# Two attention stages and the join between them: query chunks outermost, three of four chunks joined inside the first attention, units issued ahead of weighted sums in the second

## The chip, the core and the metric

The kernel runs on one core of a Trainium2 chip. The core has TensorE (matmuls into eight PSUM banks), VectorE, ScalarE, GpSimd and SyncE, each with its own instruction stream; semaphores order them. The metric is the device time of one execution in microseconds, the median of three.

## The reference, cut to what matters

```python
# x: (1, 2048, 128) f32; everything f32
xn = layernorm(x)
# s: first attention, 16 heads of 8, relu instead of softmax, no mask
qkv = xn @ w_qkv                       # per head: q, k, v of 8 columns each
w = relu(q @ k.T / sqrt(8));  w = w / (sum(w) + 1e-6)
y = xn + (w @ v, heads joined) @ w_out + b_out
s = (y - mean(y)) * rsqrt(var(y) + 1e-5) * gamma + beta
# g: a routed transformer block over 255 selected tokens
g = silu(routed_block(xn))
x = x + s * g
xn = layernorm(x)
# s: second attention, 16 heads of 64, causal softmax
q, k, v = xn @ W_Q + b_Q, xn @ W_K + b_K, xn @ W_V + b_V
s = sum over heads of softmax(causal(q @ k.T / 8)) @ v @ W_O, + b_O
# FFN with int32 weights, HIDDEN = 384
g = silu((silu(xn @ w_gate.T) * (xn @ w_up.T)) @ w_down.T)      # weights scaled by 1/127
return x + s * g
```

## The kernel before

Five functions run one after the other, each a block in which every engine has its own program: `prepare`, `routed0`, `attention0`, `between`, `attention1`. The 2048 tokens are 16 tiles (T) of 128, or 4 chunks (NC) of 512 (C = 512 columns, one PSUM bank). Activations stay in SBUF throughout: `sh.x` the residual, `sh.xa` the normalized input, `sh.g` the gate.

**First attention (`attention0`).** Heads are in four groups of four (G = GH = 4). q and k of a group sit in `q_rows` and `k_rows`, copied from DRAM in 16 loads of 128 KB a group by `load_rows` (a load is one `dma_start` at L246 or L249). Group 0 was loaded in `routed0`; groups 1 to 3 are loaded by SyncE at the start of this block, ahead of the weights for the join. A turn is one group and one chunk of queries, 16 turns, group outermost; a step is one tile of 128 keys, 16 steps a turn. In a step TensorE fills two pairs of banks with scores (`scores(s, 0)` and `(s, 1)`, L346), pairs taken from a ring of three, and then adds the weighted sums of the step two earlier (`weigh(s - LAG)`, L363). Of each pair ScalarE makes one relu tile (L406), VectorE the other (L434):

```python
if n >= RING:
    pe.wait_ge(act_relu, n - RING + 1)
    pe.wait_ge(dve_relu, n - RING + 1)
```

Once a turn ScalarE copies the summed output of the turn before (`copy_out`, L397), TensorE turns it by four transposes (L372), and VectorE divides by the sums in three small instructions (`divide`, L418 to L423). GpSimd copies the v columns of each group (two buffers) and folds `beta`, `gamma` and `b_out` into `sh.x`, `sh.g` and `sh.xa`.

**Join and FFN (`between`).** Everything waits for the last turn. TensorE turns the attention's output back (16 matmuls against the identity), ScalarE copies it, TensorE multiplies by `w_out`; VectorE adds `sh.xa` and takes the moments of all 16 tiles, ScalarE takes one square root (L1101), VectorE refines it by a Newton step (`rsqrt_refine`, L65), ScalarE scales 16 tiles (L1124), GpSimd multiplies by `sh.g` and adds to `sh.x` (L1144). Then the second layernorm in two halves, in the same manner, and per chunk four transposes, a split of the turned input in a high and a low part (`x_high`, `x_low`), three gate units (L1082), the multiply into `inner` (L1197), the down projection (L1062) and the last silu (L1118).

**Second attention (`attention1`).** Eight laps, one pair of heads each. A lap has 40 steps (query chunk and tile of 128 keys, causal), in ten groups of four (PER = 4). Units are what fills a pair of banks from a ring of three: `scores` (L1525, L1528), `maximum` (scores once more for the row maxima, L1477, L1482, taken by VectorE at L1687), `turn` and `project`, `value`, `mix`, the "whole" units of the next chunk or lap. `MAXIMA` says how many maxima a group holds, `WHOLE` which whole units. TensorE, ScalarE and VectorE all walk this list; TensorE's loop is

```python
for k in range(GROUPS):
    for unit in rows_phase(k):       # scores and maxima
        fill(unit)
    if k - 1 in ENDS:
        total(ENDS.index(k - 1))
    for s in range(k * PER, (k + 1) * PER):
        weigh(s)                     # weighted sums of the four steps
    for unit in whole_phase(k):
        fill(unit)
```

ScalarE does the exponentials (L1630) and the high parts of projections (`k_hi`, L1609), VectorE the low parts (`k_lo` L1676, `q_lo` L1679) and, after each of a lap's four query chunks, the reciprocal of the row sums and the product with it (`scale`, L1708 and L1711). GpSimd adds up the exponentials (L1444) and sets masks and constants at the start of the block (from L1391 on), which TensorE waits for before its first unit.

Of the kernel before, what the change touches and what calls it, by code (L numbers as in the profile page):

```python
# [15 lines left out]
P = 128  # L16
# [223 lines left out]
def load_rows(sp, sh, group, q_rows, k_rows, loaded):  # L240

    for h in range(GH):
        head = slice((group * GH + h) * HD0, (group * GH + h + 1) * HD0)
        for n in range(PARTS):
            rows = slice(h * ROWS0 + n * PARTS * HD0, h * ROWS0 + (n + 1) * PARTS * HD0)
            sp.dma_start(q_rows[rows, :].bitcast(F32),  # L246
                         sh.parts_dram[0, n, head, :].unsqueeze(0).to_broadcast([PARTS, HD0, S]))\
                .then_inc(loaded, 16)
            sp.dma_start(k_rows[rows, :].bitcast(F32), sh.parts_dram[1, :, head, :]).then_inc(loaded, 16)  # L249


def attention0(nc, a, sh):

    with ExitStack() as ctx:
# [7 lines left out]
        NB = 2  # L262
# [4 lines left out]
        q_rows = [sh.q_rows] + [sb(f"q_rows{n}", [P, S], F32R) for n in range(1, G)]  # L267
        k_rows = [sh.k_rows] + [sb(f"k_rows{n}", [P, S], F32R) for n in range(1, G)]
        v_cols = [sh.v_cols] + [sb(f"v_cols{n}", [P, T, GH, VW]) for n in range(1, NB)]
        w = sb("w0", [P, WR, GH, C])  # L270
        o_sb = sb("o_sb", [P, C])
        den = sb("den", [P, TC, GH])
        beta_g = sb("beta_g", [P, T, D])

        rows_loaded = [sh.rows_loaded] + [sem(f"rows_loaded{n}") for n in range(1, G)]
        fold_step = sem("fold_step")
        v_copied = sem("v_copied")
# [7 lines left out]
        out_done = sem("out_done")  # L285

        bank = sh.bank
        pair_bank = [bank[2 * n:2 * n + 2] for n in range(RING)]
        out_bank = bank[2 * RING:2 * RING + 2]

# [3 lines left out]
        def _(sp):  # L294

            for group in range(1, G):
                load_rows(sp, sh, group, q_rows[group], k_rows[group], rows_loaded[group])
# [6 lines left out]
            sp.dma_start(sh.w_int[:, 2, :], a["L1_ffn_w_down"]).then_inc(sh.join_loaded, 16)  # L304

        @block.gpsimd
        def _(pool):
# [5 lines left out]
            def fold():  # L313

                pool.wait_ge(sh.join_loaded, 16 * 7)
                link(nc.gpsimd.tensor_tensor(beta_g[:, :, :], sh.g[:, :, :], row(2), ALU.mult))
                link(nc.gpsimd.tensor_tensor(sh.x[:, :, :], sh.x[:, :, :], beta_g[:, :, :], ALU.add))
                link(nc.gpsimd.tensor_tensor(sh.g[:, :, :], sh.g[:, :, :], row(1), ALU.mult))
                link(nc.gpsimd.tensor_tensor(sh.xa[:, :, 0:D], sh.xa[:, :, 0:D], row(0), ALU.add))

            for n in range(1, NB):
                nc.gpsimd.memset(v_cols[n][:, :, :, HD0 + 1:VW], 0.0)
                nc.gpsimd.memset(v_cols[n][:, :, :, HD0:HD0 + 1], 1.0)
            for group in range(1, G):
                if group == NB:
                    fold()
                if group >= NB:

                    pool.wait_ge(weighted, (group - NB + 1) * NC * T)
                heads = sh.v0[:, :, group * GH * HD0:(group + 1) * GH * HD0]  # L330
                nc.gpsimd.tensor_copy(v_cols[group % NB][:, :, :, 0:HD0],
                                      heads.rearrange("p t (h j) -> p t h j", j=HD0)).then_inc(v_copied, 1)

        @block.tensor
        def _(pe):
            def scores(s, m):

                turn, kt = divmod(s, T)
                group, qc = divmod(turn, NC)
                n = 2 * s + m  # L340
                if n >= RING:
                    pe.wait_ge(act_relu, n - RING + 1)
                    pe.wait_ge(dve_relu, n - RING + 1)
# [6 lines left out]
            def weigh(s):  # L350
                turn, kt = divmod(s, T)
                group = turn // NC

                pe.wait_ge(act_relu, 2 * s + 2)
                pe.wait_ge(dve_relu, 2 * s + 2)
                if kt == 0:
                    if turn % NC == 0 and group:
# [1464 lines left out]
```

## Time and profile before

| | us |
|---|---|
| median of three runs | 1516.79 |
| the three runs | 1518.03, 1516.79, 1513.65 |
| the profiled execution | 1512.94 |
| its span | 1511.10 |
| TensorE busy | 1343.0 (89%) |
| VectorE busy | 1066.3 (71%) |
| ScalarE busy | 713.9 (47%) |
| GpSimd busy | 690.5 (46%) |

The span is the time from the first to the last instruction of the profiled execution; the 1.84 us between it and that execution's own time lie around the program. The busy times are averages over stages with different limits: the first attention runs from 158.3 to 545.9 us, the join and FFN to 618.3, the second attention to the end, and each is read by itself. The granted TensorE clock is a share of full speed. The chain of work that ended last runs over TensorE for 41% of the span, VectorE 10%, GpSimd and ScalarE 3% each.

### The profile page before, as it was taken

To read this page: it belongs to the slowest core of one execution; us is meant where nothing else is said; L and a number is where in the kernel's file an instruction comes from. 1 tells how busy PE (TensorE), PEld (TensorE's weight loads), DVE (VectorE), ACT (ScalarE), POOL (GpSimd) and SP (SyncE) were. 2 spreads that over 40 slices of the span, in tenths; PEclk is the share of its full clock that TensorE was granted. 3 is DMA by queue.
4 is the path that set the end of the run, shared out by engine and by line. 5 is a ranking of instruction groups with operands and counts; after the bars stand their busy time and mean duration, and the time that the engine had idled before them with its cause. 6 is when DMAs were issued, how large, how long until landed. Compare 5 with 4: busy or idle time off the path is not lost.

```text
span 1511.1 us, 25889 instructions
## 1 busy us (share of the span) xinstructions
PE 1343.0 (89%) x10066; PEld 700.4 (46%) x10066; DVE 1066.3 (71%) x1631; ACT 713.9 (47%) x1134; POOL 690.5 (46%) x485
## 2 busy tenths in 40 slices
PE   5398999999999964598999999999999999999894
PEld 3377322222222233455555555555555555555552
DVE  6774788888888866377676586586676765765853
ACT  2043677777777753333434434444434344344431
POOL 1100000400000002155777777877777777777785
PEclk9598999999999997999999999999999999999997
DMA  5100111100000010000000000000000000000000
GB/s 183 65 8 0 41 54 59 40 1 2 2 1 2 2 43 1 16 1 1 1 2 1 1 1 1 1 1 1 1 1 1 1 1 1 2 1 1 8 8 14
DMA packets 18183, 21.59 MB, mean 14 GB/s; under 512 B 7672, under 2 KB 15888, under 8 KB 16528
## 3 DMA queue, kind: packets, MB, share of 16 engines
q1 hardware_dynamic: 18064, 19.94, 3.8%
q8 instruction: 82, 1.34, 0.4%
q14 instruction: 37, 0.30, 0.1%
HBM read 14.70 MB, written 5.24 MB: 13 GB/s over the span
## 4 chain that ended last, share of the span: by engine, by line
PE 41%; DVE 10%; POOL 3%; ACT 3%; issue 1%; POOLq 0%; DVEq 0%; ACTq 0%
PE psum L1547 14%; PE psum L1525 11%; PE psum L1477 4%; DVE part_max L1687 4%; PE psum L1528 3%; POOL acc L1444 3%; PE psum L1509 2%; DVE inv L1708 2%; ACT prob L1630 2%; PE psum L1500 2%; DVE k_lo L1676 2%; ACT k_hi L1609 1%; DVE q_lo L1679 1%; PE psum L1464 1%; PE psum L1455 1%; PE psum L1457 1%
## 5 line engine op out<-in xcount | busy, mean ns | idle before, releaser
L1444 POOL TENSOR_TENSOR acc<-acc,prob 128x1024 f32<-128x1024 f32 (+3 forms) x264 | 525.3, 1990 | 91.3 <-ACT prob L1630 59.9
L1687 DVE TENSOR_REDUCE part_max<-psum 128x2 f32<-128x1024 f32 (+2 forms) x320 | 334.9, 1064 | 105.5 <-PE psum L1477 81.1
L1630 ACT ACTIVATE prob<-psum 128x1024 f32<-128x1024 f32 (+1 forms) x320 | 283.0, 897 | 210.7 <-PE psum L1528 205.5
L434 DVE TENSOR_SCALAR w<-psum 128x512 f32<-128x512 f32 x512 | 328.1, 686 | 49.8 <-PE psum L346 33.6
L406 ACT ACTIVATE w<-psum 128x512 f32<-128x512 f32 x512 | 278.0, 596 | 102.7 <-PE psum L346 102.5
L363 PE MATMUL psum<-w,v_cols 128*32 128x512 f32 x2048 | 273.6, 607 | 0.0
L1547 PE MATMUL psum<-prob,v_pair 128*64 128x512 f32 (+3 forms) x1280 | 251.3, 535 | 5.7 <-POOL prob L1414 5.7
L1525 PE MATMUL psum<-q_hi,k_hi 64*128 64x512 f32 (+3 forms) x640 | 138.8, 429 | 34.0 <-DVE q_lo L1679 23.0
L1547 PEld LDWEIGHTS psum<-prob,v_pair 128*64 128x64 f32 x1280 | 87.8, 137 | 148.8 <-issue 130.2
L1477 PE MATMUL psum<-k_hi,q_hi 64*128 64x512 f32 (+3 forms) x640 | 129.3, 402 | 16.2 <-DVE max_rows L1702 5.5
L1708 DVE RECIPROCAL inv<-psum 128x512 f32<-128x512 f32 x32 | 107.4, 3355 | 28.2 <-PE psum L1500 27.9
L1525 PE MATMUL psum<-q_hi,k_lo 64*128 64x512 f32 (+3 forms) x640 | 117.9, 363 | 0.0
L1525 PE MATMUL psum<-q_lo,k_hi 64*128 64x512 f32 (+3 forms) x640 | 117.8, 362 | 0.0
L1528 PE MATMUL psum<-max_rows,ones_r 64*128 64x512 f32 (+3 forms) x640 | 117.6, 362 | 0.0
L346 PEld LDWEIGHTS psum<-q_rows,k_rows 32*128 32x128 f32 x768 | 41.0, 181 | 156.3 <-ACT w L406 148.7
L346 PE MATMUL psum<-q_rows,k_rows 32*128 32x512 f32 x768 | 104.6, 493 | 0.0
L1525 PEld LDWEIGHTS psum<-q_hi,k_hi 64*128 64x128 f32 x640 | 60.2, 184 | 89.8 <-DVE q_lo L1679 31.1
L1144 POOL TENSOR_TENSOR y<-y,g 128x512 f32<-128x512 f32 x4 | 5.1, 1265 | 210.5 <-ACT y L1124 210.5
L1414 POOL TENSOR_SCALAR_AFFINE_SELECT prob<-prob 128x256 f32<-128x256 f32 x128 | 51.8, 406 | 107.1 <-ACT prob L1630 106.0
L1477 PEld LDWEIGHTS psum<-k_hi,q_hi 64*128 64x128 f32 x640 | 60.6, 185 | 63.1 <-ACT prob L1630 36.3
L1609 ACT ACTIVATE k_hi<-psum,bias 128x512 fp32r<-128x512 f32 x32 | 22.0, 689 | 122.5 <-PE psum L1457 122.5
L1440 POOL TENSOR_TENSOR acc<-prob 128x1024 f32<-128x1024 f32 x24 | 57.3, 2386 | 32.0 <-ACT prob L1630 30.4
(268 smaller groups left out, 1460.5 us busy)
## 6 DMA issues: line engine op xcount, KB each, us to landing
parts_dram<-parts SPq DMA_DIRECT2D x4, 1024.0 KB, 4.7
q_rows<-parts_dram SPq DMA_DIRECT2D x24, 128.0 KB
k_rows<-parts_dram SPq DMA_DIRECT2D x24, 128.0 KB
x<-in_L_attn_x SPq DMA_DIRECT2D x4, 256.0 KB, 3.9
mask<-in_L_ffn_attention_mask SPq DMA_DIRECT2D x1, 1024.0 KB, 5.4
x_high<-parts_dram SPq DMA_DIRECT2D x8, 128.0 KB
x_low<-parts_dram SPq DMA_DIRECT2D x8, 128.0 KB
out<-xa SPq DMA_DIRECT2D x4, 256.0 KB, 2.3
```

The lines of the kernel that those rows point to most:

```text
L346: last = nc.tensor.matmul(pair_bank[n % RING][i], k_rows[group][rows, kt * P:(kt + 1) * P], q_rows[group][rows, qc * C:(qc + 1) * C], star ...
L363: last = nc.tensor.matmul(out_bank[turn % 2][h * VW:(h + 1) * VW, :], v_cols[group % NB][:, kt, h, :], w[:, s % WR, h, :], start=(kt == 0) ...
L406: nc.scalar.activation(w[:, s % WR, 2 * m, :], pair_bank[n % RING][0], ACT.Relu)\
L434: nc.vector.tensor_scalar(w[:, s % WR, 2 * m + 1, :], pair_bank[n % RING][1], 0.0, None, ALU.max)\
L1444: nc.gpsimd.tensor_tensor(sums, sums, prob[:, s % PR, :, q0:C], ALU.add).then_inc(summed, 1)
L1477: last = nc.tensor.matmul(to[:, m, 0:n], q_hi[HALF[m], i * P:(i + 1) * P], k_hi[hp % 2][HALF[m], c * C:c * C + n], start=True, stop=not di ...
L1525: nc.tensor.matmul(to[:, m, q0:C], left[HALF[m], keys], right[HALF[m], at], start=n == 0, stop=False)
L1528: last = nc.tensor.matmul(to[:, m, q0:C], ones_r[HALF[m], :], max_rows[HALF[m], at], start=False, stop=True)
L1547: last = nc.tensor.matmul(out_bank[HALF[m], q0:C], v_pair[hp % 2][:, kt, HALF[m]], prob[:, s % PR, m, q0:C], start=kt == 0, stop=kt == (qc ...
L1630: nc.scalar.activation(prob[:, s % PR, :, q0:C], unit_both[n % RING][:, :, q0:C], ACT.Exp, scale=SCALE)\
L1687: nc.vector.tensor_reduce(part_max[:, :, i, c], unit_both[n % RING][:, :, 0:cols], AX_X, ALU.max)\
L1708: nc.vector.reciprocal(inv[:, :], side_bank).then_inc(inv_done, 1)
```

## The change

**Row loads.** Group 1 is loaded in `routed0` by SyncE, behind the other loads of that block. In `attention0` SyncE loads group 3 alone, and ScalarE's program begins with the 16 loads of group 2. The loads of the second attention's head weights, of `row_o` and of `wo` move from later blocks to the end of SyncE's list in `attention0`.

```diff
         @block.sync
         def _(sp):
-            for group in range(1, G):
-                load_rows(sp, sh, group, q_rows[group], k_rows[group], rows_loaded[group])
+            load_rows(sp, sh, 3, q_rows[3], k_rows[3], rows_loaded[3])
...
+            load_heads_start(sp, a, sh)
...
         @block.scalar
         def _(act):
+            load_rows(act, sh, 2, q_rows[2], k_rows[2], rows_loaded[2])
```

ScalarE's instructions at the start of the first attention, before (the two branches open the block, `w` are relu tiles):

```order
L444 UNCONDITIONAL_BRANCH
L390 UNCONDITIONAL_BRANCH
L406 ACTIVATE w<-psum 128x512 x36
L397 COPY o_sb<-psum 128x512
L406 ACTIVATE w<-psum 128x512 x32
```

and after (the two DMA rows stand there eight times in turn):

```order
L593 UNCONDITIONAL_BRANCH
L499 UNCONDITIONAL_BRANCH
L246 DMA q_rows<-parts_dram 16x1x2048
L249 DMA k_rows<-parts_dram 16x1x2048
...
L529 ACTIVATE w<-psum 128x512 x37
L508 COPY o_sb<-psum 128x512
L529 ACTIVATE w<-psum 128x512 x34
```

Sixteen DMAs stand ahead of the first relu, and the rows of 32 relu tiles a turn have become 34.

**Turns.** The query chunk is outermost, the group innermost, so that a chunk has all its heads after four turns. v columns have a buffer for each group. In listed steps (`SPARE`) ScalarE makes both relu tiles of the step's second pair and VectorE none: the divide step, step 12 of each turn, and the steps in which VectorE works for the join. The waits count accordingly.

```diff
-                group, qc = divmod(turn, NC)
+                qc, group = divmod(turn, G)
                 n = 2 * s + m
                 if n >= RING:
-                    pe.wait_ge(act_relu, n - RING + 1)
-                    pe.wait_ge(dve_relu, n - RING + 1)
+                    pe.wait_ge(act_relu, ACTS[n - RING])
+                    pe.wait_ge(dve_relu, DVES[n - RING])
...
+        DIVIDE = LAG + 2
+        TURN_O, COPY_O, MIX_O = 7, 8, 10
+        SUM, STATS, VARIANCE, REFINE = 11, (15, 19), 22, 26
+        STATS_X, VARIANCE_X, REFINE_X = (38, 42), 46, 50
+        JOIN = {turn * T: turn // G - 1 for turn in range(G, TURNS, G)}
+        AFTER = {s: (c, s - first) for first, c in JOIN.items() for s in range(first, first + G * T)}
+        DVE_FULL = (SUM,) + STATS + (REFINE,) + STATS_X + (REFINE_X,)
+        SPARE = [s for s in range(STEPS)
+                 if s % T == DIVIDE and s >= T or s in AFTER and AFTER[s][1] in DVE_FULL or s % T == 12]
+        ON_ACT = [2 * s + 1 for s in SPARE]
```

**Joins inside.** For the chunks 0, 1 and 2 the join runs within the next chunk's turns, at the offsets of the list above in steps from the turn's start: transposes (TensorE), a copy (ScalarE), the product with `w_out` (TensorE), sum and moments, a square root (ScalarE), the Newton step (VectorE), the scaling, the product with `sh.g` and the sum (GpSimd, `join_result`), then the second layernorm in the same way.

```diff
+            def turn_rows(c):
+                pe.wait_ge(out_done, (c + 1) * G)
+                for j in range(TC):
+                    last = nc.tensor.transpose(out_bank[1][:, j * P:(j + 1) * P], sh.o0[:, c % 2, j, :], sh.ident[:, :])
...
+            def mix(c):
+                pe.wait_ge(oT_done, c + 1)
+                pe.wait_ge(folded, 1)
+                for j in range(TC):
+                    last = nc.tensor.matmul(out_bank[1][:, j * P:(j + 1) * P], oT[:, j * P:(j + 1) * P], sh.w_out[:, :],
...
+def join_refine(nc, link, sh, n, at, scaled):
+    rsqrt_refine(link, nc, sh.rstd[:, n, at], sh.root[:, n, at], sh.var_eps[:, n, at], sh.newton[:, at])
+    return nc.vector.scalar_tensor_tensor(out=sh.shift[:, n, at], in0=sh.moments[:, n, at, 0], scalar=-1.0,
...
+def join_result(nc, link, sh, c, x_done):
+    for t in range(c * TC, (c + 1) * TC):
+        last = nc.gpsimd.tensor_scalar(sh.xa[:, t, 0:D], sh.xa[:, t, 0:D], sh.rstd[:, 0, t:t + 1],
+                                       sh.shift[:, 0, t:t + 1], ALU.mult, ALU.add)
+    link(last)
+    link(nc.gpsimd.tensor_tensor(sh.xa[:, at, 0:D], sh.xa[:, at, 0:D], sh.g[:, at, :], ALU.mult))
+    nc.gpsimd.tensor_tensor(sh.x[:, at, :], sh.x[:, at, :], sh.xa[:, at, 0:D], ALU.add).then_inc(x_done, 1)
```

GpSimd also runs `second_constants` there, the masks, `ident_b`, `ones_r` and `own_tile` of the second attention.

**`between`.** Only the last chunk is joined here. Its chain (copy, transposes, divide, transposes, copy, product, sum, square root, scaling on GpSimd, second layernorm) is interleaved with the FFN of chunks 0 to 2; chunk 3's FFN ends the block. TensorE's order, in the names of the new code:

```diff
+            turn_xn(0)
...
+            turn_xn(1)
...
+            gate(0, 0)
...
+            gate(0, 1)
+            gate(0, 2)
+            turn_xn(2)
+            for f in range(F1T):
+                gate(1, f)
+            down(0)
+            for f in range(F1T):
+                gate(2, f)
+            down(1)
+            turn_xn(3)
+            down(2)
+            for f in range(F1T):
+                gate(3, f)
+            down(3)
```

ScalarE from the weights' copies in this block on, before:

```order
L1095 COPY wT<-psum 128x384
L1101 ACT_TABLE_LOAD
L1101 ACTIVATE root_j<-var_eps_j 128x16
L1124 ACTIVATE y<-y,shift_j,rstd_j 128x128 x16
L1101 ACTIVATE root_j<-var_eps_j 128x8 x2
L1131 CAST w_high<-w_heads 128x2048
L1105 CAST x_high<-psum 128x512
L1106 COPY xnT<-psum 128x512
L1111 ACT_TABLE_LOAD
L1111 ACTIVATE act_gate<-psum 128x512 x3
```

and after:

```order
L1277 COPY wT<-psum 128x384
L1279 COPY o0T_last<-psum 128x512
L1262 ACT_TABLE_LOAD
L1262 ACTIVATE act_gate<-psum 128x512
L1254 CAST x_high<-psum 128x512
L1255 COPY xnT<-psum 128x512
L1262 ACTIVATE act_gate<-psum 128x512 x2
L1250 ACT_TABLE_LOAD
L1250 ACTIVATE root_j<-var_eps_j 128x4
...
L1262 ACT_TABLE_LOAD
```

The sixteen scalings (`y`) are gone from ScalarE, and square roots alternate with silu, each change of function behind a table load.

**Second attention.** The constants' wait on TensorE is gone. Whole units come ahead of the weighted sums, and of everything that follows a chunk's end:

```diff
             for k in range(GROUPS):
                 for unit in rows_phase(k):
                     fill(unit)
+                for unit in whole_phase(k):
+                    fill(unit)
                 if k - 1 in ENDS:
                     total(ENDS.index(k - 1))
                 for s in range(k * PER, (k + 1) * PER):
                     weigh(s)
-                for unit in whole_phase(k):
-                    fill(unit)
```

The same exchange is made on ScalarE (ahead of `copy_out`) and VectorE (ahead of `scale`). `MAXIMA` becomes 3, 5, 2, 5, 5, 2, 5, 5, 5, 3 instead of four a group; `PLACES` says where in a group they stand (mostly one ahead of each score unit), and `WHOLE` is dealt anew. `neg_max` gets two buffers.

VectorE around one scaling in the first full lap, before:

```order
L1687 TENSOR_REDUCE part_max<-psum 128x2 x4
L1708 RECIPROCAL inv<-psum 128x512
L1711 TENSOR_TENSOR z<-z,inv 128x512
L1676 SCALAR_TENSOR_TENSOR k_lo<-psum,bias,k_hi 128x512
L1679 SCALAR_TENSOR_TENSOR q_lo<-psum,bias,q_hi 128x512
L1687 TENSOR_REDUCE part_max<-psum 128x2 x4
L1695 TENSOR_REDUCE neg_max<-part_max 128x2x4
```

and after:

```order
L1829 TENSOR_REDUCE part_max<-psum 128x2 x5
L1818 SCALAR_TENSOR_TENSOR k_lo<-psum,bias,k_hi 128x512
L1821 SCALAR_TENSOR_TENSOR q_lo<-psum,bias,q_hi 128x512
L1850 RECIPROCAL inv<-psum 128x512
L1853 TENSOR_TENSOR z<-z,inv 128x512
L1829 TENSOR_REDUCE part_max<-psum 128x2 x5
L1837 TENSOR_REDUCE neg_max<-part_max 128x2x4
```

The reciprocal and its product stood ahead of the low parts and now stand behind them, right in front of the next maxima.

## Rows read from the trace of the kernel before

**Rows 1.** Windows: stretch, length, busy (instructions) by engine, clock, DMA share, GB/s.

```profile
158.30:254.70 96.40, 95.51 (x766) 24.83 (x767) 83.14 (x137) 70.28 (x131) 1.97 (x3) 0.98 0.13 53
...
544.70:618.30 73.60, 38.28 (x345) 31.19 (x341) 37.25 (x126) 28.43 (x54) 9.99 (x8) 0.81 0.10 23
...
858.60:964.80 106.20, 100.56 (x734) 59.02 (x732) 72.26 (x68) 44.85 (x56) 80.03 (x54) 1.00 0.00 1
```

**Rows 2.** Timeline, first attention: start, us, engine, line, operation, out<-in, [idle before <-releaser].

```profile
188.32 0.66 PE L372 MATMUL psum<-ident,o_sb 128*128 128x128 f32 x4
...
190.73 0.16 DVE L418 TENSOR_SCALAR den<-psum 128x16 f32<-128x16 f32 x1
...
191.42 2.47 DVE L434 TENSOR_SCALAR w<-psum 128x512 f32<-128x512 f32 x4
...
191.79 0.95 PE L346 MATMUL psum<-x_high,x_low 32*128 32x512 f32 x4
...
193.67 0.51 PE L346 MATMUL psum<-x_high,x_low 32*128 32x512 f32 x4
...
195.10 0.52 PE L346 MATMUL psum<-x_high,x_low 32*128 32x512 f32 x4
...
195.71 1.08 ACT L406 ACTIVATE w<-psum 128x512 f32<-128x512 f32 x2 [0.35 <-PE psum L346]
```

**Rows 3.** Timeline of SyncE's queue, first attention.

```profile
158.30 0.62 SPq L246 DMA_DIRECT2D q_rows<-parts_dram  x1
...
165.36 2.12 SPq L249 DMA_DIRECT2D k_rows<-parts_dram  x1
...
173.96 2.11 SPq L249 DMA_DIRECT2D k_rows<-parts_dram  x1
...
253.05 2.11 SPq L249 DMA_DIRECT2D k_rows<-parts_dram  x1
```

**Rows 4.** Timeline of the join and FFN, all engines.

```profile
545.94 0.58 ACT L397 COPY o_sb<-psum 128x512 f32<-128x512 f32 x1 [1.60 <-PE psum L363]
...
553.89 1.28 ACT L1101 ACT_TABLE_LOAD   x1
...
562.33 0.25 DVE L65 RECIPROCAL rstd_j<-root_j 128x16 f32<-128x16 f32 x1 [0.28 <-ACT root_j L1101]
...
563.66 6.26 ACT L1124 ACTIVATE y<-y,shift_j,rstd_j 128x128 f32<-128x128 f32 x16 [1.37 <-DVE shift_j L1176]
...
565.39 1.26 POOL L1144 TENSOR_TENSOR y<-y,g 128x512 f32<-128x512 f32 x1 [210.53 <-ACT y L1124]
...
590.87 2.94 PE L1062 MATMUL psum<-wT,inner 128*128 128x128 f32 x24 [0.97 <-DVE inner L1197]
...
594.58 0.40 PE L1082 MATMUL psum<-x_high,wT_int 128*128 128x512 f32 x1
...
594.81 0.40 PE L1082 MATMUL psum<-x_low,wT_int 128*128 128x512 f32 x1
```

**Rows 5.** Timeline, start of the second attention, TensorE.

```profile
625.94 0.77 PE L1455 MATMUL psum<-x_high,w_high 128*128 128x512 f32 x1 [7.18 <-POOLq L1407]
```

**Rows 6.** Who waited for whom, one lap, 858.6 to 964.8: total us, times, longest.

```profile
PEld psum L1477 <- ACT prob L1630: 5.0, 14, 0.5
...
PEld psum L1525 <- DVE q_lo L1679: 4.6, 4, 1.3
PEld psum L1525 <- DVE part_max L1687: 3.9, 12, 0.7
...
PEld psum L1477 <- DVE max_rows L1702: 1.2, 1, 1.2
```

**Rows 7.** Timeline of VectorE in the same lap.

```profile
903.19 3.36 DVE L1708 RECIPROCAL inv<-psum 128x512 f32<-128x512 f32 x1
906.58 1.97 DVE L1711 TENSOR_TENSOR z<-z,inv 128x512 f32<-128x512 f32 x1
...
913.26 1.23 DVE L1687 TENSOR_REDUCE part_max<-psum 128x2 f32<-128x1024 f32 x1 [0.17 <-PE psum L1477]
```

More of the change, by code:

```diff
@@ new lines, in turn_xn, with gate @@
+                    last = nc.tensor.transpose(bank[c][:, j * P:(j + 1) * P], sh.xa[:, c * TC + j, 0:D], sh.ident[:, :])
+                last.then_inc(xn_turned, 1)
+            def gate(c, f):
+                n = c * F1T + f
+                if f == 0:
+                    pe.wait_ge(x_low_done, c + 1)
+                if n == 0:
+                    pe.wait_ge(wT_done, 3)
+                if n == 1:
+                    pe.wait_ge(out_done, 1)
+                if n >= 2:
+                    pe.wait_ge(inner_done, n - 1)
+                for m in range(2):
+                    for part in (sh.x_high, sh.x_low):
+                        last = nc.tensor.matmul(gate_bank[n % 2][m], wT_int[:, m, f * P:(f + 1) * P],
+                                                part[:, c * C:(c + 1) * C], start=part is sh.x_high,
+                                                stop=part is sh.x_low)
+                last.then_inc(gate_done, 1)
@@ new lines, in _ @@
+            turn_xn(1)
+            pe.wait_ge(out_done, 1)
+            for j in range(TC):
+                last = nc.tensor.transpose(bank[LAST][:, j * P:(j + 1) * P], sh.o0[:, LAST % 2, j, :], sh.ident[:, :])
+            last.then_inc(o_turned, 1)
+            gate(0, 0)
+            pe.wait_ge(oT_done, 1)
+            for j in range(TC):
+                last = nc.tensor.matmul(bank[LAST][:, j * P:(j + 1) * P], oT[:, j * P:(j + 1) * P], sh.w_out[:, :],
+                                        start=True, stop=True)
@@ L1088, in _, with deviation @@
+            last.then_inc(projected, 1)
+            gate(0, 1)
[12 more added lines that the diff above has]
+            down(3)
         @block.scalar
         def _(act):
-            for c in range(NC):
-                act.wait_ge(turned, c + 1)
-                nc.scalar.copy(oT[:, c * C:(c + 1) * C], bank[c]).then_inc(oT_done, 1)
+            def deviation(n):
+                at = slice(LAST * TC, T)
+                act.wait_ge(var_done, n + 1)
+                nc.scalar.activation(sh.root[:, n, at], sh.var_eps[:, n, at], ACT.Sqrt).then_inc(root_done, 1)
@@ L1128, in _ @@
-            for m in range(PARTS_X):
-                deviation(1, m)
+            act.wait_ge(o_turned, 1)
+            nc.scalar.copy(oT[:, :], bank[LAST]).then_inc(oT_done, 1)
+            gate(0, 0)
+            take_xn(1)
+            gate(0, 1)
+            gate(0, 2)
+            deviation(0)
+            take_xn(2)
+            for f in range(F1T):
+                gate(1, f)
+            gate(2, 0)
+            finish(0)
+            deviation(1)
+            gate(2, 1)
+            gate(2, 2)
@@ L1194, in multiply @@
[L1194 to L1204 removed]
+            at_last = slice(LAST * TC, T)
@@ L1653, in _ @@
                     take(unit)
+                for unit in whole_phase(k):
+                    take(unit)
                 if k in ENDS:
                     copy_out(ENDS.index(k))
-                for unit in whole_phase(k):
-                    take(unit)
         @block.vector
```

584 lines of the change are left out of this document (315 added, 269 removed).

## The prediction, made before the changed kernel had run

> **What bounds the kernel now.** I read the windows by stage first, then the timeline inside each stage, then who waited for whom. The program is four stages in a row: preparation and the routed block to 158.3 us, the first attention from 158.3 to 545.9, the join with its FFN to 618.3, the second attention to the end. In the two attention stages TensorE is busy nearly all the time; in the join its busy share is 38.28 of 73.60 us and its granted clock 0.81 [rows 1]. That stage is a chain through all engines, not a load.
>
> In the first attention a step is two pairs of score tiles, four relu tiles and one set of weighted sums. TensorE sets the pace: steps start 1.43 us apart (193.67 to 195.10). Once a turn of 16 steps there are two longer ones: the output transposes at 188.32 add some 0.6 us, and the step from 191.79 to 193.67 takes 1.88, 0.45 too much, because VectorE has just done the three divide instructions that begin at 190.73 beside its two relu tiles, at 0.62 to 0.69 us each [rows 2]. VectorE is busy 83 of 96 us there and ScalarE 70 [rows 1].
>
> The row loads from DRAM are cheap only because SyncE has nothing else to do. SyncE issues 48 of them: the first eleven take 0.6 us each, from the twelfth on each issue is held 2.1 us or longer, and the 16th is through at 176.07, 17.8 us after the start. From 165.36 to 253.05 are 36 loads, 2.43 us each [rows 3]. The DMA share of that window is 0.13 of 16 engines, so about two engines carry all of it [rows 1].
>
> In the second attention a lap of one head pair takes 106.2 us, with GpSimd busy 80 [rows 1]. TensorE's queue stood 14.7 us of it: 5.0 for ScalarE's exponentials, 4.6 for the low part of a projection, 3.9 for VectorE's maxima, 1.2 for spread maxima [rows 6].
>
> **The change part by part.** The sum is made against the profiled execution, 1512.94 us (span 1511.10 and 1.84 around it). The median of the three runs shown is 3.85 higher; I carry the difference over to it.
>
> (a) Sixteen row loads, of group 2, now stand on ScalarE's own queue ahead of its first relu, while SyncE issues the 16 of group 3. No row shows a DMA issued by ScalarE, so this is bounded. By SyncE's rows, a 16th issue completes when seven loads have drained: 7 x 2.43 = 17.0, and 17.8 was seen [rows 3]. If ScalarE's loads drain through the same two engines as SyncE's, taking turns, seven of its own are 14 in all: 14 x 2.43 = 34 us. I take this, because two engines carried all loads though they go to different partitions and some nine of them were queued; that speaks for the shape of the transfer choosing the engines. Less the 0.6 us after which ScalarE's first relu started before, it is **+33**. Nothing covers it: TensorE can fill three pairs of banks, then it waits for ScalarE. The other ends are 16 x 0.62 = 9.9 us if no queue fills, and 23 x 2.43 = 56 if both queues share one stock of nine loads. A short hold would not be all gain: all 32 loads need 78 us on two engines, and turn 2, which reads group 2, would come 50 us after the first relu.
>
> The Trainium skill, "DMA: Bandwidth & Descriptors", section "Why a DMA increments its semaphore by 16 and not by 1", says that a transfer from SyncE or ScalarE runs on the lowest-numbered k engines, k following from the slowest dimensions, and both engines' DMAs run on the same 16 ("Issuing engines are not separate DMA queues"). By that rule sharing is sure. The trace agrees so far, with its two busy engines. That last section also says that a second issuer saves "the time on the sequencer it takes to initiate the DMA, which is usually small relative to the DMA itself"; by that the hold would be small and the time rival B's. SyncE's 2.11 us speaks against it.
>
> (b) The rest of the first attention. ScalarE takes both tiles of a pair in the divide step, so VectorE does one relu less where it divides (2.47/4 = 0.62 us against the 0.69 from 190.73 to 191.42, [rows 2]): 15 stalls of 0.45 go, -6.8. ScalarE has that time (0.35 us idle in a 1.43 us step, [rows 2]), and its late tile is wanted only two steps later. Three of four chunks are now joined inside: on TensorE four transposes (0.6) and four fp32 matmuls, eight passes at 2.94/24 = 0.12 [rows 4], about 1.0: 3 x 1.6 = +4.7. On VectorE the sum and the statistics are covered by the relu tiles given away; the two refinements a chunk take 1.33 us each (562.33 to 563.66, [rows 4]) against one tile of 0.62, the two variances about 0.6 against none. Where a divide of 0.69 cost 0.45, I take 0.3 for each of these 12: +3.5, between 0 and 7. One activation table load (1.28, [rows 4]) before the first square root: +1. Together **+2**. GpSimd's part and the SyncE loads behind it lie beside relu work.
>
> (c) The join and FFN take 618.3 - 545.9 = 72.4 us now: 545.94 is ScalarE's copy after the last weighted sums [rows 4], 618.3 the next block. The first down projection starts only at 590.87, 45 us in. After the change three chunks are normalized already and only the last goes through the chain, beside the FFN of the others. I follow it from the last weighted sum: copy, transposes and divide 3 us; its transposes behind nine weight transposes, one gate unit (four matmuls 0.23 apart, [rows 4]) and the mixing: 6; sum and statistics 9; square root behind a table load 10.7; refinement 13; four scalings and two products of 1.26 on GpSimd [rows 4] 17; second statistics 18.6; second root, behind two table switches and the first down projection, 22.2; 23.5; GpSimd 25; transposes 25.5; ScalarE's w_high and copies 28.4; three gate units and their multiplies 34.6; down 2.94; last activation and block end: 38.4. I add 2.5 for VectorE instructions beside GpSimd and for a TensorE clock that may sink again. 41 against 72.4: **-31**, from -36 to -27. ScalarE loads five tables here instead of two; two of the three extra ones are in this chain.
>
> (d) Constants of the second attention are set during the first. TensorE's first projection waited 7.18 us for them and then ran at the lower clock (0.77 us instead of 0.40 for a matmul) [rows 5]. The wait goes, and about 1 us of slow matmuls: **-8**.
>
> (e) Units in front of weighted sums. A projection now has 3.5 us of weighted sums behind it while ScalarE and VectorE split it, so the 4.6 and the 1.2 of [rows 6] go. But VectorE now meets the reciprocal last: 3.36 us, then a product of up to 1.97 [rows 7], start only after the whole units, and the next group's maxima stand behind them. In the group after a scaling, with q_lo done 2.3 us after the projection (k_hi, k_lo and q_lo in a row), the scaling ends 7.0 to 7.6 after it and the weighted sums 4.6: 2.4 to 3 us late. With 1.23 us a maximum and a ring of three bank pairs, the second score unit waits for the first maximum, so this lateness becomes TensorE's. I get 2.4, 1.2, 2.4 to 3 and 1.3 us for the four scalings of a lap, but the usual 0.8 of such a group is in them: about +5 net. Five maxima in full groups and two or three in diagonal ones about even out. 5.8 against 5: per lap nothing within 1.5, over eight laps **0, from -12 to +14**.
>
> Sum: 33 + 2 - 31 - 8 + 0 = -4 us: 1508.9 for the profiled run, **1513** by the median.
>
> **The rivals.** A, ScalarE's loads drain beside SyncE's on other engines: held 17.8 us, 16 less, 1497. Against it is the 0.13 share [rows 1]. A2, the second attention gains 2 us a lap: GpSimd is busy 80 of 106, so there is room [rows 1], and a late maximum may fall into a place where TensorE waited for ScalarE anyway (5.0, [rows 6]): 1497. B, no queue fills: 9.9 us of issue, on other engines, 1489; SyncE's twelfth load [rows 3] speaks against it. C, slower: the reciprocal behind the whole units costs more than the projections give back. Place: the group after each scaling; price 2 us a lap, 1529; it decides once the first maximum after a scaling starts over 3 us after its matmuls. D, slower: the two queues share one stock of queued loads, the hold is 56 us, 1535; it decides when ScalarE's issues are held before its tenth. That the change doesn't do what it says would be the divide stalls and the 7.18 wait still standing; the order of instructions leaves no room for it.
>
> **How the numbers follow.** A measurement here tells about 0.3%, 4.6 us, from no change. Forecast 0.40, with its own range 1505 to 1521; A 0.17; A2 0.13; B 0.04; C 0.16; D 0.07; 0.03 elsewhere. The forecast lies on the border: of its 0.40, 0.18 are faster by over 4.6 us, 0.16 within, 0.06 slower. Faster 0.18 + 0.16 + 0.12 + 0.04 + 0.01 = 0.51; within 0.19; slower 0.30. The range 1488 to 1534 leaves out D and the tails.
>
> **What would show it.** Right: ScalarE's first relu 30 to 37 us after the first attention's start, two DMA engines busy till then; no 1.88 us steps in a turn; 38 to 44 us from the last weighted sums of the first attention to the second attention's block, its first projection within 1 us of it; laps of 105 to 108 us, with no wait for q_lo and longer ones for maxima after each reciprocal. Wrong: a first relu before 20 us or after 50, laps under 104 or over 108, or waits of TensorE for the square roots' chain.

## The result and the profile after

| | before | after |
|---|---|---|
| median, us | 1515.22 | 1497.99 |
| ratio, with its 95% interval | | 0.9892, 0.9862 to 0.9922 |
| profiled execution, us | 1512.94 | 1502.96 |
| its span | 1511.10 | 1501.2 |

The change makes the kernel 1.1% faster, 17 us by the medians. The profiled execution of after is its slowest: the other three took 1496.8 to 1498.5. By stage of the two profiled executions (from the last weighted sums of the first attention, and from the first projection of the second):

| stage | before | after | difference |
|---|---|---|---|
| preparation and routed block | 158.3 | 164.6 | +6.3 |
| first attention | 387.6 | 424.4 | +36.8 |
| to the first projection: join, FFN, constants | 80.1 | 37.7 | -42.3 |
| second attention | 885.2 | 874.4 | -10.7 |
| sum | 1511.1 | 1501.2 | -9.9 |

The first line is mostly not the change's. In the profiled executions of the experiments below, which all have the changed routed block, it took 158.0 to 164.7 us; before has one profile, 158.3. Whether the loads of group 1, which now stand in that block, cost a part of it stays open.

ScalarE's queue at the start of the first attention of after, in order of time, and under it SyncE's in the same stretch:

```profile
164.65 1.44 ACTq L246 DMA_DIRECT2D q_rows<-parts_dram  x1
...
171.78 3.46 ACTq L249 DMA_DIRECT2D k_rows<-parts_dram  x1
175.27 4.26 ACTq L246 DMA_DIRECT2D q_rows<-parts_dram  x1
...
196.74 4.56 ACTq L249 DMA_DIRECT2D k_rows<-parts_dram  x1
201.35 3.06 ACT L529 ACTIVATE w<-psum 128x512 f32<-128x512 f32 x6 [36.96 <-issue]
```

```profile
172.15 8.91 SPq L249 DMA_DIRECT2D k_rows<-parts_dram  x1
181.10 4.25 SPq L246 DMA_DIRECT2D q_rows<-parts_dram  x1
```

Nine loads go out at 0.6 to 0.8 us (the very first at 1.4), then the other seven are held, 3.46 to 4.56 us, most of them 4.26, twice the 2.11 of [rows 3]: the two queues take turns. ScalarE's first relu starts 36.7 us after the first load. Windows of after (columns as in [rows 1]) say what the machine does meanwhile, what became of the join, and give one lap of the second attention:

```profile
170.00:180.00 10.00, 0.00 (x0) 0.00 (x0) 0.00 (x0) 0.00 (x0) 0.41 (x1) 0.50 0.13 54
...
589.03:626.50 37.47, 28.96 (x186) 23.98 (x186) 19.57 (x54) 23.83 (x37) 6.41 (x11) 1.00 0.00 1
...
858.57:963.56 104.99, 100.97 (x733) 60.53 (x733) 69.79 (x68) 45.19 (x57) 79.59 (x54) 0.98 0.00 1
```

From 170 to 180 no compute engine works but GpSimd, for 0.4 us, and the DMA share is still 0.13: 32 loads from two queues move no more than 48 from one did [rows 1]. The join stage is half as long as in [rows 1], at full clock instead of 0.81. The lap is 105.0 instead of 106.2.

Inside the first attention, the timeline of TensorE around a divide and around the join of chunk 0:

```profile
280.39 0.52 PE L433 MATMUL psum<-q_rows,k_rows 32*128 32x512 f32 x4
...
281.83 0.51 PE L433 MATMUL psum<-q_rows,k_rows 32*128 32x512 f32 x4
...
283.26 0.53 PE L433 MATMUL psum<-q_rows,k_rows 32*128 32x512 f32 x4
```

```profile
306.95 0.50 PE L433 MATMUL psum<-x_high,x_low 32*128 32x512 f32 x4
307.39 1.06 PE L453 MATMUL psum<-w,v_cols 128*32 128x512 f32 x8
308.38 0.66 PE L470 MATMUL psum<-ident,o 128*128 128x128 f32 x4
308.97 0.51 PE L433 MATMUL psum<-x_high,x_low 32*128 32x512 f32 x4
```

The step with the divide takes 1.43 us; the 1.88 of [rows 2] is gone. The transposes for the join make one step 2.02. A turn without a join takes 23.6 us instead of 24.04.

The chain of the last chunk in the join, in order of time: copy, scaling on GpSimd, second square root, first gate unit of the last chunk, first projection of the second attention.

```profile
589.37 0.59 ACT L1273 COPY o_sb<-psum 128x512 f32<-128x512 f32 x1 [1.86 <-PEq L315]
...
600.88 1.73 POOL L278 TENSOR_SCALAR xa<-xa,rstd_j,shift_j 128x128 f32<-128x128 f32 x4 [30.10 <-DVE shift_j L270]
...
610.06 0.20 ACT L1250 ACTIVATE root_j<-var_eps_j 128x4 f32<-128x4 f32 x1
...
617.43 0.50 PE L1191 MATMUL psum<-x_high,wT_int 128*128 128x512 f32 x1 [0.73 <-DVE x_low L1319]
...
626.76 0.50 PE L1598 MATMUL psum<-x_high,w_high 128*128 128x512 f32 x1
```

In the second attention, one scaling of a lap of after: reciprocal, product, the next maximum, and TensorE's next matmuls. They answer to [rows 7].

```profile
867.20 3.36 DVE L1850 RECIPROCAL inv<-psum 128x512 f32<-128x512 f32 x1 [1.41 <-PE psum L1643]
...
870.59 1.17 DVE L1853 TENSOR_TENSOR z<-z,inv 128x512 f32<-128x512 f32 x1
...
871.68 1.21 DVE L1829 TENSOR_REDUCE part_max<-psum 128x2 f32<-128x1024 f32 x1
872.95 0.50 PE L1668 MATMUL psum<-q_hi,k_hi 64*128 64x512 f32 x2 [1.87 <-DVE part_max L1829]
...
873.80 0.67 PE L1671 MATMUL psum<-max_rows,ones_r 64*128 64x512 f32 x2
```

The second score unit waits 1.87 us for the maximum that stands behind the reciprocal, as the prediction described. After the wait matmuls take 0.67 us instead of 0.40, and the window of those 3.4 us shows the clock at 0.54, the lower of its two levels:

```profile
873.40:876.80 3.40, 3.40 (x21) 2.78 (x19) 2.17 (x2) 1.19 (x2) 1.20 (x1) 0.54 0.00 0
```

The 1.87 us wait stands in each of seven laps that I followed; the slow matmuls follow it in five of them. Such a lap is 105.0 to 105.3 us; the one from 1068.8 to 1172.7, without them, is 103.9. Who waited for whom in a lap of after (853 to 958) answers to [rows 6]; PE rows are waits of matmuls, PEld rows those of the loads of their weights, and the numbers are total, times and longest. No row for q_lo is left; VectorE's maxima have grown:

```profile
PEld psum L1668 <- DVE part_max L1829: 6.4, 11, 2.3
...
PE psum L1668 <- DVE part_max L1829: 3.1, 4, 1.9
PEld psum L1620 <- ACT prob L1772: 2.5, 8, 0.4
```

### The profile page after: what moved, and what is told of

Its sections match the earlier page's. It is cut to its first block, busy times and chain, and to the rows that moved or that the text cites. A ratio compares the mean times of both kernels' runs of the same rounds, so it can differ in the third digit from the quotient of the medians.

```text
span 1501.2 us, 25720 instructions
## 1 busy us (share of the span) xinstructions
PE 1342.9 (89%) x9954; PEld 707.8 (47%) x9954; DVE 1018.8 (68%) x1600; ACT 735.3 (49%) x1179; POOL 704.7 (47%) x521
## 4 chain that ended last, share of the span: by engine, by line
PE 40%; DVE 10%; ACT 3%; POOL 2%; issue 1%; POOLq 0%; ACTq 0%
PE psum L1690 12%; PE psum L1668 11%; DVE part_max L1829 4%; PE psum L1620 4%; DVE inv L1850 4%; PE psum L1671 3%; ACT prob L1772 2%; PE psum L1652 2%; PE psum L1607 2%; POOL acc L1587 2%; PE psum L1643 2%; PE psum L1598 1%; DVE z L1853 1%; PE psum L1600 1%; PE psum L1599 1%; PE psum L1625 1%
## 5 line engine op out<-in xcount | busy, mean ns | idle before, releaser
L578 DVE TENSOR_SCALAR w<-psum 128x512 f32<-128x512 f32 x460 | 297.9, 686 | 100.8 <-PE psum L433 88.2
L529 ACT ACTIVATE w<-psum 128x512 f32<-128x512 f32 x564 | 298.5, 602 | 116.1 <-PE psum L433 78.7
L1620 PE MATMUL psum<-k_hi,q_hi 64*128 64x512 f32 (+3 forms) x640 | 132.4, 410 | 6.0 <-DVE part_max L1829 4.4
L278 POOL TENSOR_SCALAR xa<-xa,rstd_j,shift_j 128x128 f32<-128x128 f32 x16 | 6.9, 448 | 213.9 <-DVE shift_j L270 213.9
L433 PE MATMUL psum<-q_rows,k_rows 32*128 32x512 f32 x768 | 101.1, 492 | 0.1
L453 PEld LDWEIGHTS psum<-w,v_cols 128*32 128x32 f32 x2048 | 40.6, 108 | 63.6 <-ACT w L529 53.5
```

The lines of the kernel that those rows point to most:

```text
L433: last = nc.tensor.matmul(pair_bank[n % RING][i], k_rows[group][rows, kt * P:(kt + 1) * P], q_rows[group][rows, qc * C:(qc + 1) * C], star ...
L453: last = nc.tensor.matmul(out_bank[turn % 2][h * VW:(h + 1) * VW, :], v_cols[group][:, kt, h, :], w[:, s % WR, h, :], start=(kt == 0), sto ...
L529: nc.scalar.activation(w[:, s % WR, 2 * m + i, :], pair_bank[n % RING][i], ACT.Relu)\
L578: nc.vector.tensor_scalar(w[:, s % WR, 2 * m + 1, :], pair_bank[n % RING][1], 0.0, None, ALU.max)\
L1620: last = nc.tensor.matmul(to[:, m, 0:n], q_hi[HALF[m], i * P:(i + 1) * P], k_hi[hp % 2][HALF[m], c * C:c * C + n], start=True, stop=not di ...
```

## The experiments

The medians before beside these runs were 1517 to 1519 us, against 1515 beside the changed kernel. Times of experiments stand against the changed kernel's 1498, and by themselves differences under some 5 us say nothing.

### Where the 36.7 us of ScalarE come from

**Group 2's loads back on SyncE.**

```diff
-            load_rows(sp, sh, 3, q_rows[3], k_rows[3], rows_loaded[3])
+            for group in (2, 3):
+                load_rows(sp, sh, group, q_rows[group], k_rows[group], rows_loaded[group])
...
-            load_rows(act, sh, 2, q_rows[2], k_rows[2], rows_loaded[2])
```

> The changed kernel with the 16 row loads of group 2 back on SyncE, ahead of group 3's; ScalarE issues none. Theory (the hold is the drain of ScalarE's own queue through the two engines that SyncE's loads use): the first relu comes within 1 us of the block's start, so 36 us go; all 32 loads drain in 32 x 2.43 = 78 us, turn 3 wants group 3 some 71 us in, so 5 to 8 us come back as a wait there: 28 to 31 us less than the changed kernel. Rival (the hold only moved a wait that TensorE would have for the rows anyway): within 5 us of the changed kernel.

Measured: 1473.3 us, ratio to before 0.9707 (0.9679 to 0.9735), 25 us less than the changed kernel. ScalarE's first relu of its profile, and who waited for whom at turn 3:

```profile
160.38 2.56 ACT L529 ACTIVATE w<-psum 128x512 f32<-128x512 f32 x5 [0.82 <-PE psum L434]
```

```profile
PEld psum L434 <- DMA k_rows<-parts_dram: 10.8, 1, 10.8
PE psum L434 <- DMA k_rows<-parts_dram: 9.9, 1, 9.9
```

The hold is gone and a wait of 9.9 us for group 3's rows took its place; 5 to 8 were expected. Two slow steps behind it (2.7 and 2.6 us instead of 1.43) cost 2.4 more. So 25 of the 36 us come back by the issuer alone, and the rest is the rate of the loads.

**Each load cut in two**, 8 partitions instead of 16, 32 issues on each of the two queues:

```diff
-            queue.dma_start(q_rows[rows, :].bitcast(F32),
-                         sh.parts_dram[0, n, head, :].unsqueeze(0).to_broadcast([PARTS, HD0, S]))\
-                .then_inc(loaded, 16)
-            queue.dma_start(k_rows[rows, :].bitcast(F32), sh.parts_dram[1, :, head, :]).then_inc(loaded, 16)
+            for m in range(PARTS):
+                eight = slice(rows.start + m * HD0, rows.start + (m + 1) * HD0)
+                queue.dma_start(q_rows[eight, :].bitcast(F32), sh.parts_dram[0, n, head, :]).then_inc(loaded, 16)
+                queue.dma_start(k_rows[eight, :].bitcast(F32), sh.parts_dram[1, m, head, :]).then_inc(loaded, 16)
```

> The changed kernel with each row load cut into two of 8 partitions with 2048 columns (64 KB), 32 issues on ScalarE and 32 on SyncE. Theory (the shape's outermost size chose two engines): now eight engines carry them, no issue is held, ScalarE is busy for 32 x 0.6 = 19 to 21 us and the time falls by 15 to 18 us. Rival (two engines belong to these queues whatever the shape): the bytes are the same, so the hold stays 34 to 38 us and the time stays, or grows with the number of issues.

Measured: 1493.3 us, from 1483.1 (the profiled one) to 1498.1, ratio 0.9851 (0.9812 to 0.9890). The time can't be told from the changed kernel's, and the 15 to 18 us expected are not there; the profile can. Its first attention is 12.2 us shorter (412.2 against 424.4); the other three executions took 1491 to 1498 us, and what they lost is open. An issue on ScalarE, the first relu, and the wait at turn 2:

```profile
159.63 0.28 ACTq L249 DMA_DIRECT2D k_rows<-parts_dram  x1
...
170.33 3.06 ACT L529 ACTIVATE w<-psum 128x512 f32<-128x512 f32 x6 [11.58 <-issue]
```

```profile
228.78 0.90 PE L433 MATMUL psum<-q_rows,k_rows 32*128 32x512 f32 x4 [11.40 <-DMA k_rows<-parts_dram]
```

No issue is held, and each takes 0.3 us, so the hold is 11.6 us. But the rows don't come soon enough: turn 2 would start 58 us into the block and waits 11.4 us for group 2, which shares the rate with group 3. Its last packet starts 68 us in, in the changed kernel 81. The windows from 180 to 200 us, first of the changed kernel with SyncE's uncut loads, then of these cut ones:

```profile
180.00:200.00 20.00, 20.00 (x168) 5.21 (x172) 16.75 (x29) 15.64 (x31) 0.00 (x0) 1.00 0.13 55
```

```profile
180.00:200.00 20.00, 20.00 (x168) 5.06 (x160) 17.37 (x27) 15.88 (x30) 0.00 (x0) 1.00 0.55 68
```

The DMA share goes from 0.13 to 0.55, two engines to eight or nine, and the rate from 55 to 68 GB/s. The shape does choose the number of engines, but four times the engines carry the bytes 1.24 times as fast: single packets of 8 KB took 0.309 us with two in flight and 1.05 on average (median 1.17) with eight. Of the 68 GB/s, 62 are the rows'; the others belong mostly to the loads that stand behind them.

**The cut loads on SyncE alone**, both edits above.

> The changed kernel with groups 2 and 3 on SyncE and each row load cut into two of 8 partitions (64 issues in all, none on ScalarE). The run with cut loads on both queues showed packets of 8 KB that took 1.2 us with eight in flight, against 0.309 us with two: the bytes went little faster. Theory (cut loads bring 60 to 68 GB/s against 54): group 2 is there after 31 to 35 us, group 3 after 62 to 70, before turn 3 wants it at 71; the wait of 10 us that the uncut SyncE version has at turn 3 goes, and with it the slow clock behind it: 1460 to 1464. Rival (the rate stays at 54 GB/s): the wait stays, 1470 to 1475.

Measured: 1461.5 us, ratio 0.9645 (0.9609 to 0.9680). Turn 3 no longer waits for rows: its longest step there is 1.76 us instead of 1.43. The first attention of its profile takes 388.0 us, 36.4 less than the changed kernel's and 0.4 more than before: the whole hold was to be had. The rate in the same window:

```profile
180.00:200.00 20.00, 20.00 (x168) 5.03 (x160) 17.49 (x30) 15.62 (x30) 0.00 (x0) 1.00 0.55 72
```

**The same loads issued over the four heads first**, so that those in flight together write partitions 32 apart:

```diff
-    for h in range(GH):
...
+    for n in range(PARTS):
+        for m in range(PARTS):
+            for h in range(GH):
```

> As the cut loads on SyncE, but the order of issue goes over the four heads first, so that the loads in flight together write partitions 32 apart instead of the same or neighbouring ones. Theory (eight packets at once take 1.2 us each because they meet in one group of 32 destination partitions): packets get shorter than 0.8 us and the last row lands within 50 us. Rival (source or something common bounds them): packets stay at 1.1 to 1.2 us. The time is 1458 to 1464 by either, since turn 3 starts 71 us in.

Measured: 1463.8 us, ratio 0.9650 (0.9611 to 0.9688), a median packet of 1.20 us in this window against 1.15 with the order before, and the rate no higher:

```profile
180.00:200.00 20.00, 20.00 (x172) 5.23 (x164) 16.91 (x29) 16.01 (x31) 0.00 (x0) 1.00 0.54 65
```

So it doesn't help that loads that follow each other go to different heads. That neighbouring destinations don't bound the rate is not shown: one load still writes 8 neighbouring partitions, and the eight packets in flight may all be of one load. Destination, source or something common: which it is stays open.

### The divide step

```diff
-                 if s % T == DIVIDE and s >= T or s in AFTER and AFTER[s][1] in DVE_FULL or s % T == 12]
+                 if s in AFTER and AFTER[s][1] in DVE_FULL or s % T == 12]
```

> The changed kernel with the divide step taken off the list of steps in which ScalarE makes both tiles of the second pair. Theory (a divide of 0.69 us beside two tiles costs TensorE 0.45 us): 15 steps of 1.88 instead of 1.43 us come back, 6 to 8 us: 1504 to 1506. Rival (the stall is absorbed elsewhere): the time stays within 2 us and no step of 1.8 us is seen.

Measured: 1504.0 us, ratio 0.9902 (0.9864 to 0.9941), 6 more than the changed kernel by the medians, which the intervals don't tell from none. The profile does: the first attention takes 431.3 us against 424.4, 6.9 more, where the five other runs that leave this stage as it is are within 0.8 us of 424.4. A divide step, 1.89 us long:

```profile
231.19 0.97 PE L433 MATMUL psum<-q_rows,k_rows 32*128 32x512 f32 x4
...
233.08 0.50 PE L433 MATMUL psum<-q_rows,k_rows 32*128 32x512 f32 x4
```

### What gave the second attention its 10.7 us

**The old order under the new tables**: weighted sums, row sums, scaling and copy ahead of the whole units, on three engines.

```diff
-                for unit in whole_phase(k):
-                    fill(unit)
                 if k - 1 in ENDS:
                     total(ENDS.index(k - 1))
                 for s in range(k * PER, (k + 1) * PER):
                     weigh(s)
+                for unit in whole_phase(k):
+                    fill(unit)
```

> The changed kernel with the second attention's old order (weighted sums, scaling and copies ahead of the whole units) under the new tables of maxima and whole units. Theory (the order took away the waits for the low parts): the waits for q_lo come back, 1.0 to 1.3 us for each of four projections a lap, less some 2 us now lost behind the reciprocals: laps 1 to 3 us longer than the changed kernel's 105.0, 8 to 24 us in all. Rival (the tables gave the gain): laps stay within 0.5 us of 105.0, the time within 4.

Measured: 1535.2 us, ratio 1.0116 (1.0086 to 1.0145), 37 more than the changed kernel, above the 8 to 24 expected, so the rival (the tables gave the gain by themselves) is refuted; a lap is 108.6 us and shows the wait for q_lo again:

```profile
PEld psum L1668 <- DVE q_lo L1821: 4.1, 3, 1.8
...
PE psum L1668 <- DVE q_lo L1821: 3.3, 3, 1.6
```

**The old tables under the new order**: `WHOLE` as before and four maxima in every group, one ahead of each score unit.

```diff
-        MAXIMA = [8, 6, 6, 8, 8] + [(3, 5, 2, 5, 5, 2, 5, 5, 5, 3)[k % LAPS] for k in range(5, GROUPS - 5)] + [0] * 5
-        PLACES = {0: (0, 0, 0, 0, 0), 2: (1, 0, 1, 0, 0), 3: (1, 1, 0, 1, 0), 5: (1, 1, 1, 1, 1),
+        MAXIMA = [8, 6, 6, 8, 8] + [4 for k in range(5, GROUPS - 5)] + [0] * 5
+        PLACES = {0: (0, 0, 0, 0, 0), 4: (1, 1, 1, 1, 0), 2: (1, 0, 1, 0, 0), 3: (1, 1, 0, 1, 0), 5: (1, 1, 1, 1, 1),
```

> The changed kernel with the old tables of maxima (four a group) and whole units under the new order. Theory (order gave the gain): laps within 1 us of 105.0, time within 8. Rival (tables gave the gain): laps 106 to 108, 8 to 24 us longer, because four maxima in a diagonal group or behind a reciprocal are more than its score units leave room for.

Measured: 1529.4 us, ratio 1.0096 (1.0059 to 1.0133), 31 more than the changed kernel, above the rival's 8 to 24 too; the lap is 108.9. "Order gave the gain" is refuted: the waits for maxima are what grew.

```profile
PEld psum L1668 <- DVE part_max L1829: 10.7, 17, 2.0
...
PE psum L1668 <- DVE part_max L1829: 5.7, 10, 1.6
```

**Only the maxima as before**, the new `WHOLE` kept:

> The changed kernel with four maxima in every group, and its own new list of whole units and order. With both tables old the lap is 108.9 against 105.0. Theory (the number of maxima a group carries the difference: fewer where score units are narrow or a reciprocal stands): laps 107.5 to 109, 1520 to 1530. Rival (the places of the whole units carry it): laps 105 to 106, 1498 to 1506.

Measured: 1520.0 us, ratio 1.0010 (0.9988 to 1.0032); the lap in its profile is 107.0, between both expectations. Of the second attention's time, first projection to end, the old tables have 904.1 us, this one 895.5, the changed kernel 874.4: under the new order the list of whole units is worth 8.6, the counts of maxima with their places 21.1 (by the medians 9.4 and 22.0).

**The order alone**, with the whole list of units as before, each maximum behind its score unit (`rows_phase`, `MAXIMA` and `WHOLE` of the kernel before).

> The changed kernel with the second attention's list of units wholly as before (four maxima a group, each behind its score unit, the old whole units); only the new order remains: whole units ahead of weighted sums, row sums and scaling. It took 885 us in the kernel before and 904 with the old tables but maxima ahead of score units. Theory (the order without its tables costs, because the reciprocal comes right in front of the next maxima): 890 to 906 us from the first projection to the end, 1514 to 1530 in all. Rival (the order gains by itself and the 904 came from maxima standing ahead of score units): 874 to 882 us, 1498 to 1506.

Measured: 1554.4 us, ratio 1.0247 (1.0211 to 1.0282). From the first projection at 620.3 to the end at 1551.2 are 931 us against 885 before: the order alone costs 46 us, beyond the range I had given it. And not for the reason in my theory. A lap and two of its waits:

```profile
882.55:995.17 112.62, 105.91 (x734) 60.85 (x732) 69.55 (x69) 45.43 (x56) 79.58 (x53) 0.95 0.00 1
```

```profile
PE psum L1630 <- DVE neg_max L1835: 3.4, 2, 1.7
PE psum L1666 <- DVE part_max L1827: 1.0, 3, 0.5
```

Matmuls wait only 1.0 us for maxima. They wait twice, 1.7 and 1.6 us, for the row maxima of a tile put together (`neg_max`), which the lap before [rows 6] and the changed kernel's don't. And TensorE is busy 105.9 us at a clock of 0.95, where the lap of [rows 1] has 100.6 at 1.00: of 6.4 us a lap, 5.3 are matmuls that run slower.

**Scaling ahead of the whole units again**, units still ahead of the weighted sums:

```diff
-                for unit in whole_phase(k):
-                    take(unit)
                 if k - 1 in ENDS:
                     scale(ENDS.index(k - 1))
+                for unit in whole_phase(k):
+                    take(unit)
```

and the same with `total` on TensorE.

> The changed kernel with the row sums (TensorE) and the scaling (VectorE) back ahead of the whole units, the units still ahead of the weighted sums. Theory (the low parts ahead of the reciprocal are what frees TensorE, and the 2 us lost behind the first scaling of a lap are their price): low parts come 4 to 5 us later where a projection stands with a scaling, laps grow by 1 to 4 us, 1506 to 1530. Rival (the reciprocal behind the units is the larger loss): laps of 103 to 104, 1482 to 1490.

Measured: 1489.1 us, ratio 0.9825 (0.9795 to 0.9854), 9 less than the changed kernel. My theory was wrong and its rival right. The same place in a lap, and the lap as a window:

```profile
867.66 0.50 PE L1668 MATMUL psum<-q_hi,k_hi 64*128 64x512 f32 x2 [0.87 <-DVE part_max L1829]
...
868.47 0.39 PE L1671 MATMUL psum<-max_rows,ones_r 64*128 64x512 f32 x2
```

```profile
854.16:957.49 103.33, 100.82 (x733) 58.68 (x732) 72.89 (x68) 45.28 (x56) 79.95 (x54) 1.00 0.00 1
```

The wait is 0.87 instead of 1.87 us and the clock stays up: matmuls take 0.39, and the lap's clock is 1.00 instead of 0.98. The second attention takes 865.3 us, 9.1 less. The low parts do come later, but nobody waits long for them (0.4 and 0.3 us of a lap).

### Both gains together

Cut loads on SyncE, and the scaling ahead of the whole units.

> The changed kernel with the two edits that gained: cut row loads of groups 2 and 3 on SyncE, and row sums and scaling ahead of the whole units. They lie in different stages, so the gains should add: 1461.5 less the 9 of the scaling edit, 1450 to 1454, first relu within 1 us of the block's start, laps of 103.3. Rival (they share a cause, such as the TensorE clock of the run): under half of the 9 us shows, 1457 or more.

Measured: 1452.9 us, ratio 0.9578 (0.9540 to 0.9617), 3.0% less than the changed kernel and the fastest of the study. A lap of its profile:

```profile
850.00:953.30 103.30, 100.80 (x734) 58.74 (x734) 72.76 (x69) 45.20 (x57) 79.85 (x53) 1.00 0.00 1
```

## Why the prediction was right and wrong, step by step

The forecast was 1513, the range 1488 to 1534; 1498 lies in it, close to the times of rivals A and A2. It lies outside the likeliest case's own range, 1505 to 1521. Against the sum of -4 the stages give -16.2: (a) and (b) cost 1.8 more than forecast, (c) and (d) gave 3.3 more, (e) 10.7. The width of (e) is what keeps the result well inside the range.

- **(a), ScalarE's hold, +33: right.** It is 36.7 less the 0.6 of before. The mechanism is the one taken, two engines in turns: 4.26 us an issue is twice 2.13. It came out 2.7 longer than 34: nine unheld issues took 7.1 us by themselves, which the sum had not, and the seven held ones 29.6, which is 14 x 2.11 and not 14 x 2.43. D, the shared stock, would have been 56, and is refuted; so are A and B, by the 4.26 us. Their conditions were false; that the time of A is what was measured is luck: mostly (e) gave it. A2 came in part: 1.2 us a lap instead of its 2.
- **The Trainium skill's rule in (a)**, on the number of engines ("DMA: Bandwidth & Descriptors", "Why a DMA increments its semaphore by 16 and not by 1"): the traces agree, two engines at first and, with the outermost size at eight, a share of 0.55. The Trainium skill's remark on issue time ("Issuing engines are not separate DMA queues") did not hold for a queue that fills: 4.26 us of sequencer a load.
- **(b), the rest of the first attention, +2: right.** 36.8 less 36.1 leaves +0.7. A turn without join is 0.44 shorter, and putting the divide's relu back cost 6.9 us in the profile (6.8 forecast). Two TensorE insertions a chunk make 1.66 us (1.6 forecast); the two variances and one refinement stretch a step each by 0.25, 2.2 us in all where 3.5 were put down; the activation table load costs 0.6 once (1 forecast).
- **(c), join and FFN, -31: right, somewhat small.** From the last weighted sums to the next block's first projection are 37.7 us, with 38.4 in the chain and 2.5 added for clock and company: the clock was 1.00 throughout, and the addition was not needed. That makes -35.0.
- **(d), the constants, -8: right.** The first projection's matmul starts 0.3 us into its block instead of 7.6 and takes 0.50 us instead of 0.77.
- **(e), the second attention, 0 with -12 to +14: the step that failed, within its bounds.** It was -10.7. About 1 us of that belongs to the clock in (d). The working had 5.8 us a lap gained against 5 lost and put the 0.8 between them at nothing, 6.4 us over eight laps. The gain came: no wait for q_lo or max_rows is left in a lap. The losses behind a scaling are in the trace, but smaller: 1.87 and 0.93 us behind two of a lap's four, 3.1 in all by the matmuls' waits for maxima, where I had 2.4, 1.2, 2.4 to 3 and 1.3. The low clock behind the 1.87, 1.2 us in most laps, no term had.

  What failed most is the sentence "Five maxima in full groups and two or three in diagonal ones about even out". With maxima back at four a group the second attention takes 21 us more. It is also why C did not come: its mechanism is real (9 us by the run that undoes it), but the tables paid for it and more: with four maxima the stage takes 895.5 us, 10.3 more than before. C's sign was not met either: after the scaling shown, the first maximum starts 2.4 us after the start of its matmuls, not over 3. The 46 us of the order alone are not C's, by the waits shown there. I weighed the order and took the tables as neutral, without walking VectorE's load group by group.

The 6.3 us of the routed block in the profiled execution are no part of the account: with them the table says -9.9; the sum by stages without them, -16.2, agrees with the medians' -17.

## What to carry to other kernels

A DMA issue is an instruction of its engine: once its queue is full, an engine that computes stands for as long as the loads ahead take to drain, and a second issuer on the same two DMA engines doubled that time, from 2.11 to 4.26 us a load. Put such loads on an engine that computes nothing, and ask of the rate, not of the issuer, whether they land in time. A change of order and a change of how much work stands in each place are one change: in the second attention each without the other took 19 to 46 us more than before, together they gained 11.

## What the runs showed of the hardware that I had not expected

In windows of loads of 8 KB rows from DRAM the rate was 53 to 55 GB/s on two DMA engines (0.309 us a packet) and 65 to 72 on eight (1.0 to 1.1 us a packet on average), of which the rows were 59 to 65. An issue of a 16-partition load took 0.6 us with an empty queue, one of an 8-partition load 0.3. And TensorE's clock, after a wait of only 1.87 us, stood at its lower level for some 3 us in five of seven laps, which cost 1.2 us on top of the wait; after 0.93 us in the same laps, or 0.87 in the run with scaling ahead, it did not.
